# Openings of four stages prepared one stage earlier, and logits of a tree tile alternated with the outputs of the last one

## The chip, the cores and the metric

The kernel runs on one core of one Trainium2 chip. The metric is device time in microseconds (us), the median of three runs. A core has a matrix engine (TensorE, PE in the profile; its weight loads are shown as PEld), VectorE (DVE), ScalarE (ACT), GpSimd (POOL) and SyncE (SP), which here issues all DMA transfers. The engines run their own instruction streams and wait for each other through semaphores.

## The reference

Two transformer layers on x of shape (2, 1024, 128), all float32. In each, attention and feed-forward part read the same normalised x, and both are added to x:

```python
xn = layernorm(x)
x = x + attn0(xn) + moe(xn)      # 16 heads of 8, causal; 8 experts, top 2, hidden 512, gelu
xn = layernorm(x)
x = x + attn1(xn) + trees(xn)    # 16 query heads of 64 on 4 key heads, rotary, causal, top 64 scores
```

The tree part, which the change touches most:

```python
logits = x @ W_in.T + b_in                    # width 8 * 255: 8 binary trees of depth 7
decisions = (logits > 0)                      # at each node: left or right
acts = silu(logits)
dmap = nodes on the path from the root        # 8 of 255 per tree
out = (acts * dmap) @ W_out.T
```

## The kernel before

`build_program` (L2182) builds six stages, each an `nc.Block()` with one instruction stream per engine and a barrier of all engines at its end. Their buffers are taken at the start of a stage and given back at its end, except those in `g`, which live longer:

1. `project_layer0` (L109): layer norm, q and k of the first attention as three bf16 parts (written to DRAM by SyncE), v, router logits.
2. `attend_layer0` (L245): 32 heads. Its VectorE stream first clears q, k, v, nil and none (L654 to L661), counting on the semaphore `blank`; SyncE loads the first heads' q and k after `blank` 2 (L351), PE starts after `blank` 4 (L531).
3. `run_experts` (L667): router on VectorE, then 4 chunks of 512 tokens by 8 experts, PE and ScalarE (gelu) in turn. SyncE loads the tables of the trees at its start (L691 to L695); GpSimd has nothing to do.
4. `project_layer1` (L799): SyncE loads ten tables (L873), PE waits for all (L895), then for 16 tiles turns the attention output, multiplies it with wo and adds biases (L904 to L912), VectorE adds the sums to x. Then layer norm, v, and rotated q and k for the second attention, with GpSimd adding the two products of each rotation (L1098). VectorE clears v1, keys and second first (L1019 to L1021).
5. `walk_trees` (L1999): the trees, 16 tiles of 128 tokens.
6. `attend_layer1` (L1188): 32 heads in a software pipeline written out by hand. SyncE loads q, k and v of two heads, then seven tables (L1351); PE, GpSimd and VectorE wait for all seven (`table_in`), PE and ScalarE also for VectorE's clearing of the upper halves of q and k (`blank`).

In `walk_trees` VectorE first splits the bias `b_in` into three bf16 parts that sum to it (L2134 to L2137, on one partition), and SyncE moves these by DMA into three partitions (`bins`, L2030); PE waits for them. Then for each tile t: PE computes the logits in four chunks of 512 columns, two chunks to a half (`logits`, L2052); VectorE thresholds each half (`dec`, L2143), walks seven levels to get the path (L2151, L2152) and multiplies the activations with it ("masking", L2159, semaphore `masked`); ScalarE makes the activations of each half (`silu`, L2105). PE then turns the masked activations in four groups (`turn`, L2072, into ps_t), ScalarE copies each group to mT (`turned`, L2113), and PE multiplies it with W_out (L2083, `outputs`); VectorE adds the result to x (L2164). The order of each engine is written out: PE does logits(t), then outputs(t-1); ScalarE does both silus of t, then the four copies of t-1; VectorE does walk(t), then add(t-1). An instruction stream is in order, so that what stands behind a wait waits too.

## Time and profile before

| | |
|---|---|
| median of 3 runs | 2088.07 us (2087.74 to 2088.33) |
| profiled execution | 2088.2 us, its span 2086.5 |
| mean granted TensorE clock | 0.93 of full speed |
| PE / DVE / ACT / POOL busy | 84% / 72% / 64% / 30% of the span |

The span runs from the first to the last instruction of the trace; times in rows are counted from its start. Busy time is the union of an engine's instructions. The granted clock has two levels here, 1.00 (2.4 GHz) and 0.50 (1.2 GHz). In the profile's names `a_` is an attention stage, `p_` a projection, `ex_` the experts, `ff_` the trees, `g_` and `l_` buffers that live longer. A row of the order of time shows start, duration, engine, line, operation, output and inputs, count of merged instructions, and in square brackets how long the engine had been idle and who released it.

### The profile page before, as it was taken

What the parts mean: (1) busy time and instruction counts of PE and PEld (TensorE: products, weight loads), DVE (VectorE), ACT (ScalarE), POOL (GpSimd) and SP (SyncE); (2) the same over time, 40 slices, a digit from 0 to 9 for tenths busy, and PEclk for the clock granted to TensorE, in tenths of its full rate; (3) what the DMA queues carried; (4) which work ended last, traced back from release to release, by engine and by line L of the source; (5) the groups of instructions that cost most, each with busy time, mean ns of one, the idle gap of its engine ahead of it and who ended that gap; (6) DMA issues with size and microseconds to landing.
All of it is one profiled execution on the core that took longest, in us unless ns stands there. A gap on an engine that the chain in (4) does not pass through costs nothing. (4 is left out here: it accounts for less than half of the span.)

```text
span 2086.5 us, 35986 instructions
## 1 busy us (share of the span) xinstructions
PE 1760.6 (84%) x10131; PEld 1056.3 (51%) x10163; DVE 1497.3 (72%) x4721; ACT 1327.3 (64%) x2819; POOL 619.0 (30%) x1540
## 2 busy tenths in 40 slices
PE   5699999999978895888865888888889838988877
PEld 2345555577756443555532555555555525555544
DVE  4588888311133555777747899999999969999974
ACT  3177777533321521233347999999999939999983
POOL 0045454000000441000014444444444414444440
PEclk8599999999985997999987999999999969999988
DMA  6200000100010220000020110111100101011000
GB/s 168 82 21 22 23 23 16 41 1 0 0 50 0 81 91 31 0 0 0 0 64 11 31 32 16 31 31 31 31 24 23 31 16 28 18 31 31 21 18 15
DMA packets 38186, 61.77 MB, mean 30 GB/s; under 512 B 10225, under 2 KB 15347, under 8 KB 38004
## 3 DMA queue, kind: packets, MB, share of 16 engines
q1 hardware_dynamic: 38069, 60.51, 9.8%
q8 instruction: 36, 0.59, 0.1%
q14 instruction: 81, 0.66, 0.1%
HBM read 34.14 MB, written 17.83 MB: 25 GB/s over the span
## 5 line engine op out<-in xcount | busy, mean ns | idle before, releaser
L1629 ACT ACTIVATE a_trash<-a_sc,a_search 128x1024 bf16<-128x1024 f32 (+7 forms) x768 | 586.2, 767 | 74.6 <-POOL a_search L1568 31.7
L1384 PE MATMUL a_ps_s<-a_k,a_q 128*128 128x512 f32 (+3 forms) x768 | 311.1, 520 | 64.4 <-DVE a_sc L1845 51.1
L1418 PE MATMUL a_ps_o<-a_kT,a_v 128*65 128x512 f32 (+3 forms) x768 | 287.5, 498 | 53.7 <-ACT a_kT L1646 52.5
L1402 PE MATMUL a_ps_t<-g_ident,a_sc 128*128 128x128 f32 x1152 | 228.5, 285 | 20.9 <-ACT a_kT L1646 18.9
L1845 DVE TENSOR_SCALAR_CACHE_REDUCE a_sc<-a_ps_s,g_search 128x1024 f32<-128x1024 f32 (+7 forms) x256 | 207.9, 812 | 23.3 <-PE a_ps_s L1386 16.1
L585 DVE TENSOR_REDUCE a_top<-a_ps_row 128x1 f32<-128x512 f32 (+3 forms) x384 | 196.7, 553 | 24.6 <-PE a_ps_row L423 18.9
L1384 PEld LDWEIGHTS a_ps_s<-a_k,a_q 128*128 128x128 f32 x768 | 132.3, 196 | 160.0 <-issue 100.6
L1805 DVE SCALAR_TENSOR_TENSOR a_below<-a_sc,a_found 128x768 f32<-128x768 f32 (+7 forms) x256 | 211.3, 835 | 1.1
L1404 PE MATMUL a_ps_t<-a_minus,a_short 128*128 128x128 bf16 x1152 | 211.8, 221 | 0.0
L1402 PEld LDWEIGHTS a_ps_t<-g_ident,a_sc 128*128 128x128 f32 x1152 | 164.5, 143 | 92.0 <-ACT a_kT L1646 47.1
L549 ACT ACTIVATE a_prob<-a_ps_col 128x1024 f32<-128x1024 f32 (+7 forms) x256 | 159.2, 650 | 68.7 <-PE a_ps_col L436 65.5
L1646 ACT ACTIVATE a_kT<-a_ps_t 128x512 f32<-128x512 f32 x288 | 162.0, 583 | 24.9 <-PE a_ps_t L1404 17.7
L1418 PEld LDWEIGHTS a_ps_o<-a_kT,a_v 128*65 128x65 f32 x768 | 89.0, 140 | 164.5 <-ACT a_kT L1646 103.3
L741 ACT ACTIVATE ex_hid<-ex_ps_h,le_b 128x512 f32<-128x512 f32 x128 | 87.5, 687 | 128.1 <-PE ex_ps_h L718 127.8
L1818 DVE MAX8 a_best<-a_below 128x8 f32<-128x160 f32 (+5 forms) x576 | 157.2, 328 | 1.1
L1629 ACT ACTIVATION_READ_ACCUMULATOR a_trash<-a_sc,a_search 128x1 f32 x768 | 148.0, 193 | 0.0
L792 DVE SCALAR_TENSOR_TENSOR l_acc<-ex_ps_y,l_comb,l_acc 128x128 f32 x112 | 31.9, 345 | 151.4 <-PE ex_ps_y L709 151.1
L1639 ACT ACTIVATE a_short<-a_sc,a_cutoff 128x128 bf16<-128x128 f32 (+2 forms) x192 | 110.8, 655 | 44.9 <-DVE a_cutoff L1865 44.9
L1404 PEld LDWEIGHTS a_ps_t<-a_minus,a_short 128*128 128x128 bf16 x1152 | 123.7, 107 | 19.4 <-issue 19.4
L709 PEld LDWEIGHTS ex_ps_y<-le_w,ex_hid 128*128 128x128 f32 x1024 | 118.7, 192 | 13.4 <-issue 13.4
L709 PE MATMUL ex_ps_y<-le_w,ex_hid 128*128 128x128 f32 x1024 | 118.8, 275 | 0.0
L420 PE MATMUL a_ps_row<-a_k,a_q 128*128 128x512 bf16 (+3 forms) x353 | 114.7, 335 | 4.8 <-DVE a_top L585 2.7
(267 smaller groups left out, 3336.1 us busy)
## 6 DMA issues: line engine op xcount, KB each, us to landing
a_v<-g_v SPq DMA_DIRECT2D x32, 260.0 KB, 2.3
q1turned<-p_full SPq DMA_DIRECT2D x32, 256.0 KB, 2.0
a_q<-q1turned SPq DMA_DIRECT2D x32, 256.0 KB, 3.6
a_k<-k1turned SPq DMA_DIRECT2D x32, 256.0 KB, 4.0
stack<-p_parts SPq DMA_DIRECT2D x24, 256.0 KB, 3.7
a_q<-stack SPq DMA_DIRECT2D x32, 96.0 KB, 2.2
a_k<-stack SPq DMA_DIRECT2D x32, 96.0 KB, 2.2
le_w<-d_w SPq DMA_DIRECT2D x1, 2048.0 KB, 8.5
```

What stands on the lines that cost most here:

```text
L549: act.activation(prob[:, p, PO[j]:PO[j] + S - j * P], ps_col[:, col_buffer(n, p, j), 0:S - j * P], ACT.Exp, scale=SCALE).then_inc(col_read, 1)
L585: dve.tensor_reduce(top[:, i, c:c + 1], ps_row[:, bank, 0:width], AX.X, ALU.max).then_inc(row_read, 1)
L709: m = pe.matmul(ps_y[:, e % 2, t, :], hid[:, e % 2, hc, t * P:(t + 1) * P], w2[:, e, hc, :], start=(hc == 0), stop=(hc == HC - 1))
L1384: pe.matmul(ps_s[:, j % 2, c:c + w], q[:, p, i * P:width], k[:, p, c:c + w], start=True, stop=True)
L1402: pe.matmul(out, columns(h, i)[:, c * P:(c + 1) * P], g.ident[:, :], is_transpose=True, start=True, stop=False)
L1404: m = pe.matmul(out, short[:, OFF[i] + c * P:OFF[i] + (c + 1) * P], minus[:, :], start=False, stop=True)
L1418: m = pe.matmul(ps_o[0:VW1, lo // HALF, (lo % HALF) * P:CH], v[:, p, c, :], kT[:, u % 2, a * P:b * P], start=(c == 0), stop=(c == LAST[lo ...
L1629: act.activation(trash[:, u % 2, 0:(i + 1) * P], columns(h, i), ACT.Sign, scale=-1.0, bias=trials[:, p, c, i:i + 1], accum_out=balance[:, ...
L1646: act.activation(kT[:, u % 2, :], ps_t[:, u % 2, :], ACT.Exp).then_inc(t_read, 1)
L1805: lane[i] = did(dve.scalar_tensor_tensor(lows(i), columns(hs, i), found[:, i:i + 1], columns(hs, i), ALU.is_le, ALU.mult))
L1818: did(dve.max(best[:, p, i, a, :], buf[:, a * w:(a + 1) * w]))
L1845: dve.tensor_scalar(columns(h + 1, i), ps_s[:, j % 2, 0:(i + 1) * P], shift.rearrange("p n i -> p (n i)"), None, ALU.subtract, ALU.max, ac ...
```

## The change

Nothing of what is computed changes. Five parts:

- First attention: its buffers q, k, v, nil and none become `g.q0`, `g.k0` and so on, and GpSimd clears them in the stage before. VectorE keeps one small memset.
- Second projection: wo, bo and b2 are loaded in the experts (`mix_in`), and PE waits for these three only, and for the other seven tables ahead of v. The three memsets go from VectorE to GpSimd; VectorE waits for them ahead of its copies of v.
- Trees: the split of the bias is made in the experts by GpSimd, and SyncE moves the parts there.
- Second attention: maskq is loaded behind the first head's q and k, with a semaphore of its own, and is all that PE waits for, beside the clearing, of which GpSimd does k and VectorE q. The other six tables are waited for in the section of head 0 (GpSimd, VectorE) and head 1 (PE).
- Trees, the order: in the section of tile t, PE does the two chunks of the first half and one of the second, waits for the masking of t-1, turns the first group of t-1, does the last chunk of t, and then the remaining turns and outputs of t-1. ScalarE puts the two silus of t between the copies of t-1. VectorE's order stays.

```diff
@@ project_layer0 @@
+
+            @block.gpsimd
+            def _(pool):
+                pool.memset(g.q0[:, :, :], 0.0).then_inc(g.blank0, 1)
+                pool.memset(g.k0[:, :, :], 0.0).then_inc(g.blank0, 1)
+                pool.wait_ge(g.blank0, 2)
+                pool.memset(g.k0[SHIFT0:SHIFT0 + NSH, :, :], 1.0).then_inc(g.blank0, 1)
+                pool.wait_ge(g.blank0, 3)
+                pool.memset(g.v0_padded[:, :, :, :], 0.0).then_inc(g.blank0, 1)
+                pool.memset(g.nil[:, :], 0.0).then_inc(g.blank0, 1)
+                pool.memset(g.none[:, :], 0.0).then_inc(g.blank0, 1)
+                pool.wait_ge(g.blank0, 6)
@@ attend_layer0 @@
-                sp.wait_ge(blank, 2)
+                sp.wait_ge(blank, 6)
...
-                pe.wait_ge(blank, 4)
+                pe.wait_ge(blank, 6)
...
-                set_up = Chain(dve, blank)
-                dve.memset(q[:, :, :], 0.0)
-                dve.memset(top[:, :, :], -3.0e38)
-                set_up(dve.memset(k[:, :, :], 0.0))
-                set_up(dve.memset(k[SHIFT0:SHIFT0 + NSH, :, :], 1.0))
-                set_up(dve.memset(v[:, :, :, :], 0.0))
-                dve.memset(none[:, :], 0.0)
-                set_up(dve.memset(nil[:, :], 0.0))
+                Chain(dve, lowest)(dve.memset(top[:, :, :], -3.0e38))
@@ run_experts @@
+                sp.dma_start(g.bin32[:, :], g.d_bin).then_inc(g.trees_in, 16)
+                for dst, src in ((g.wo0, g.d_wo0), (g.bo0, g.d_bo0), (g.b2, g.d_b2)):
+                    sp.dma_start(dst[:, :], src).then_inc(g.mix_in, 16)
                 sp.dma_start(g.win[:, :], g.d_win).then_inc(g.trees_in, 16)
-                sp.dma_start(g.bin32[:, :], g.d_bin).then_inc(g.trees_in, 16)
...
+                sp.wait_ge(bias_ready, 4)
+                for part in range(3):
+                    sp.dma_start(g.bins[part:part + 1, :], binp[0:1, part, :]).then_inc(g.bins_in, 16)
+                sp.wait_ge(g.bins_in, 48)
+
+            @block.gpsimd
+            def _(pool):
+                pool.wait_ge(g.trees_in, 64)
+                b = Chain(pool, bias_ready)
+                b(pool.tensor_copy(binp[0:1, 0, :], g.bin32[0:1, :]))
+                b(pool.tensor_tensor(rest[0:1, :], g.bin32[0:1, :], binp[0:1, 0, :], ALU.subtract))
+                b(pool.tensor_copy(binp[0:1, 1, :], rest[0:1, :]))
+                b(pool.tensor_tensor(binp[0:1, 2, :], rest[0:1, :], binp[0:1, 1, :], ALU.subtract))
@@ project_layer1 @@
-                pe.wait_ge(w_in, 16 * 10)
+                pe.wait_ge(g.mix_in, 16 * 3)
...
+                pe.wait_ge(w_in, 16 * 7)
...
-                pe.wait_ge(blank, 1)
+                pe.wait_ge(blank, 3)
...
-                dve.memset(g.v1[:, :, :, :], 1.0)
-                dve.memset(keys[:, :, :, :, P:P + 1], 1.0)
-                dve.memset(second[:, :, :, :, :], 0.0).then_inc(blank, 1)
...
+                dve.wait_ge(blank, 3)
...
-                pool.wait_ge(w_in, 16 * 10)
+                pool.memset(g.v1[:, :, :, :], 1.0).then_inc(blank, 1)
+                pool.memset(keys[:, :, :, :, P:P + 1], 1.0).then_inc(blank, 1)
+                pool.memset(second[:, :, :, :, :], 0.0).then_inc(blank, 1)
+                pool.wait_ge(blank, 3)
+                pool.wait_ge(w_in, 16 * 7)
@@ attend_layer1 @@
 
                 load(0, 0)
+                sp.dma_start(maskq[:, :], g.d_maskq1).then_inc(mask_in, 16)
+                for dst, src in ((wide[:, :], g.d_wide), (limit[:, :], g.d_limit), (ceiling[:, :], g.d_ceiling)):
+                    sp.dma_start(dst, src).then_inc(table_in, 16)
                 load(1, 1)
                 load_v(0, 0)
                 load_v(1, 1)
-                for dst, src in ((iota.rearrange("p s j -> p (s j)"), g.d_rank), (wide[:, :], g.d_wide),
-                                 (maskq[:, :], g.d_maskq1), (minus[:, :], g.d_minus), (ceiling[:, :], g.d_ceiling), (limit[:, :], g.d_limit),
+                for dst, src in ((iota.rearrange("p s j -> p (s j)"), g.d_rank), (minus[:, :], g.d_minus),
                                  (wo.rearrange("p h w -> p (h w)"), g.d_wo1)):
                     sp.dma_start(dst, src).then_inc(table_in, 16)
...
+                    if is_at(n, 1):
+                        pe.wait_ge(table_in, 16 * 6)
...
-                pe.wait_ge(blank, 3)
-                pe.wait_ge(table_in, 16 * 7)
+                pe.wait_ge(blank, 2)
+                pe.wait_ge(mask_in, 16)
...
                     if is_at(n, -1):
+                        after(did(pool.memset(k[DH1:P, :, :], 0.0)))
+                        pool.sem_inc(blank, 1)
                         did(pool.memset(inverse[:, :], -1.0))
-                        pool.wait_ge(table_in, 16 * 7)
+                    if is_at(n, 0):
+                        pool.wait_ge(table_in, 16 * 6)
                         after(did(pool.tensor_scalar(wide_aim[:, :], wide[:, :], AIM, None, ALU.add)))
...
                     if is_at(n, -1):
-                        did(dve.memset(q[DH1:P, :, :], 0.0))
-                        did(dve.memset(k[DH1:P, :, :], 0.0))
-                        after(made[0])
-                        dve.sem_inc(blank, 3)
-                        dve.wait_ge(table_in, 16 * 7)
+                        dve.memset(q[DH1:P, :, :], 0.0).then_inc(blank, 1)
                         did(dve.memset(best[:, :, NARROWEST:TB, QUARTERS, 7:8].rearrange("p b s e -> p b (s e)"), TINY))
+                    if is_at(n, 0):
+                        dve.wait_ge(table_in, 16 * 6)
                         did(dve.tensor_scalar(least[:, 0:NARROWEST], limit[:, 0:NARROWEST], TINY, None, ALU.mult))
@@ walk_trees, tensor @@
+
+                def half(t, p, x):
+                    for c, w in BOUNDS[2 * x:2 * x + 2]:
+                        pe.matmul(ps_l[:, c:c + w], g.onesb[0:3, :], bins[:, c:c + w], start=True, stop=False)
+                        yield pe.matmul(ps_l[:, c:c + w], xt[:, p, :], win[:, c:c + w], start=False, stop=True)
+
...
+                def logits(t, p, first, x, both):
                     pe.wait_ge(x_ready, t + 1)
-                    for x in range(2):
-                        if not (first and p == 0):
-                            pe.wait_ge(silu_ready, t * 2 + (x - 1))
-                        for c, w in BOUNDS[2 * x:2 * x + 2]:
-                            pe.matmul(ps_l[:, c:c + w], g.onesb[0:3, :], bins[:, c:c + w], start=True, stop=False)
-                            m = pe.matmul(ps_l[:, c:c + w], xt[:, p, :], win[:, c:c + w], start=False, stop=True)
-                        m.then_inc(l_ready, 1)
-
-                def outputs(t, p, first):
-                    pe.wait_ge(masked, t + 1)
-                    if not (first and p == 0):
-                        pe.wait_ge(f_read, t)
-
-                    def turn(x):
-                        if not (first and p == 0 and x < 2):
-                            pe.wait_ge(t_read, t * NCK + (x - 1))
-                        for c in range(4 * x, min(4 * x + 4, NCH)):
-                            w = P if c < NCH - 1 else LASTW
-                            m = pe.transpose(ps_t[0:w, x % 2, (c % 4) * P:(c % 4 + 1) * P],
-                                             act_v[:, p, c * P:c * P + w], g.ident[:, :])
-                        m.then_inc(t_ready, 1)
-
-                    turn(0)
-                    for x in range(NCK):
-                        if x + 1 < NCK:
-                            turn(x + 1)
-                        pe.wait_ge(t_read, t * NCK + (x + 1))
-                        for c in range(4 * x, min(4 * x + 4, NCH)):
-                            w = P if c < NCH - 1 else LASTW
-                            m = pe.matmul(ps_f[:, 0:P], mT[0:w, x % 2, (c % 4) * P:(c % 4 + 1) * P],
-                                          wout[0:w, c, :], start=(c == 0), stop=(c == NCH - 1))
-                        if x == NCK - 1:
-                            m.then_inc(f_ready, 1)
-
-                logits(0, 0, True)
-                logits(1, 1, True)
-                outputs(0, 0, True)
+                    if not first:
+                        pe.wait_ge(silu_ready, t * 2 + (x - 1))
+                    chunks = half(t, p, x)
+                    next(chunks)
+                    if both:
+                        next(chunks).then_inc(l_ready, 1)
+                    return chunks
+
+                def section(t, p, first):
+                    u, q = t - 1, 1 - p
+                    logits(t, p, False, 0, True)
+                    second = logits(t, p, False, 1, False)
+                    pe.wait_ge(masked, t)
+                    turn(u, q, first, 0)
+                    next(second).then_inc(l_ready, 1)
+                    turn(u, q, first, 1)
+                    output(u, q, first, 0)
+                    turn(u, q, first, 2)
+                    output(u, q, first, 1)
+                    turn(u, q, first, 3)
+                    output(u, q, first, 2)
+                    output(u, q, first, 3)
+
+                logits(0, 0, True, 0, True)
+                logits(0, 0, True, 1, True)
+                section(1, 1, True)
                 with pe.Fori(1, NT // 2) as i:
-                    logits(i * 2, 0, False)
-                    outputs(i * 2 - 1, 1, False)
-                    logits(i * 2 + 1, 1, False)
-                    outputs(i * 2, 0, False)
-                outputs(NT - 1, 1, False)
+                    section(i * 2, 0, False)
+                    section(i * 2 + 1, 1, False)
+                pe.wait_ge(masked, NT)
+                turn(NT - 1, 1, False, 0)
+                for x in range(NCK):
+                    if x + 1 < NCK:
+                        turn(NT - 1, 1, False, x + 1)
+                    output(NT - 1, 1, False, x)
 
@@ walk_trees, scalar @@
+                def section(t, p, first):
+                    u = t - 1
+                    turned(u, 0)
+                    silu(t, p, first, 0)
+                    turned(u, 1)
+                    silu(t, p, first, 1)
+                    turned(u, 2)
+                    turned(u, 3)
+
+                silu(0, 0, True, 0)
+                silu(0, 0, True, 1)
+                section(1, 1, True)
@@ walk_trees, vector @@
-                b = Chain(dve, bias_ready)
-                b(dve.tensor_copy(binp[0:1, 0, :], bin32[0:1, :]))
-                b(dve.tensor_tensor(rest[0:1, :], bin32[0:1, :], binp[0:1, 0, :], ALU.subtract))
-                b(dve.tensor_copy(binp[0:1, 1, :], rest[0:1, :]))
-                b(dve.tensor_tensor(binp[0:1, 2, :], rest[0:1, :], binp[0:1, 1, :], ALU.subtract))
-                b(dve.memset(path[:, :, 0:1], 1.0))
+                dve.memset(path[:, :, 0:1], 1.0).then_inc(bias_ready, 1)
+                dve.wait_ge(bias_ready, 1)
```

## Rows read from the trace of the kernel before

**Rows 1.** Stretches of the six stages: length, busy time by engine, clock, DMA share, GB/s.

```profile
0.00:69.00 69.00, 44.67 (x128) 28.39 (x128) 27.81 (x90) 18.26 (x30) 0.19 (x4) 0.74 0.60 174
69.00:383.00 314.00, 288.30 (x2267) 147.18 (x2299) 256.66 (x675) 217.72 (x321) 135.91 (x316) 0.96 0.08 21
383.00:612.00 229.00, 225.54 (x1288) 163.92 (x1288) 42.47 (x150) 90.01 (x131) 0.00 (x0) 1.00 0.03 10
612.00:813.00 201.00, 164.96 (x752) 91.69 (x752) 104.55 (x223) 57.04 (x144) 61.57 (x50) 0.82 0.18 66
813.00:1056.00 243.00, 191.10 (x960) 123.08 (x960) 168.95 (x301) 69.79 (x113) 5.72 (x17) 0.91 0.00 1
1056.00:2086.00 1030.00, 846.05 (x4736) 502.04 (x4736) 896.90 (x3285) 874.45 (x2081) 415.56 (x1153) 0.95 0.10 27
```

**Rows 2.** Order of time around the opening of the first attention.

```profile
74.59 3.47 DVE L658 MEMSET a_k<- 3x4096 bf16 x1 [0.91 <-DVE a_k L657]
...
78.49 0.41 SPq L349 DMA_DIRECT2D a_k<-stack  x1
...
81.02 0.29 PE L420 MATMUL a_ps_row<-a_k,a_q 128*128 128x128 bf16 x1 [0.69 <-DMA a_k<-stack]
```

**Rows 3.** Order of time, opening of the second projection.

```profile
623.52 0.48 PE L899 MATMUL p_ps_a<-g_ident,l_o 128*128 128x128 f32 x1 [12.80 <-DMA p_quantile<-d_quantile]
...
623.55 3.72 POOL L1103 TENSOR_SCALAR p_wqk<-p_wqk 128x1024 f32<-128x1024 f32 x1 [243.28 <-DMA p_quantile<-d_quantile]
...
627.24 2.76 POOL L1103 TENSOR_SCALAR p_wqk_rot<-p_wqk_rot 128x1024 f32<-128x1024 f32 x1
```

**Rows 4.** Order of time, opening of the trees.

```profile
816.19 1.51 POOL L2039 COPY ff_xt<-l_xnT 128x128 f32<-128x128 f32 x2 [18.50 <-POOLq L870]
...
827.32 0.58 PE L2058 MATMUL ff_ps_l<-ff_bins,g_onesb 3*128 3x512 bf16 x1 [17.03 <-DMA ff_bins<-ff_binp]
```

**Rows 5.** Opening of the second attention: order of time, then DMA issues (KB, us to landing).

```profile
1054.43 0.58 SPq L1339 DMA_DIRECT2D a_k<-k1turned  x1
...
1066.12 1.19 PE L1384 MATMUL a_ps_s<-a_k,a_q 128*128 128x512 f32 x1 [12.88 <-DMA a_wo<-d_wo]
...
a_k<-k1turned SPq DMA_DIRECT2D x2, 256.0 KB, 4.8
```

**Rows 6.** One tree tile in order of time.

```profile
869.24 0.38 PE L2058 MATMUL ff_ps_l<-ff_bins,g_onesb 3*128 3x512 bf16 x1
...
870.61 0.39 PE L2058 MATMUL ff_ps_l<-ff_bins,g_onesb 3*128 3x512 bf16 x1
...
873.45 1.22 DVE L2143 TENSOR_SCALAR ff_dec<-ff_ps_l 128x1016 bf16<-128x1016 f32 x1 [1.50 <-PE ff_ps_l L2059]
...
876.26 1.16 PE L2083 MATMUL ff_ps_f<-l_wout,ff_mT 128*128 128x128 f32 x8 [1.97 <-ACT ff_mT L2113]
...
880.10 2.29 DVE L2159 TENSOR_TENSOR ff_act_v<-ff_act_v,ff_path 128x2040 f32<-128x2040 f32 x1
...
882.39 0.39 PE L2058 MATMUL ff_ps_l<-ff_bins,g_onesb 3*128 3x512 bf16 x1
```

**Rows 7.** Trees: all maskings, who waited for them, first outputs, last 6.8 us.

```profile
L2159 DVE TENSOR_TENSOR ff_act_v<-ff_act_v,ff_path x16: 2282/2284/2285, 841.6 to 1044.5; 128x2040 f32<-128x2040 f32 x16
...
  PE ff_ps_t L2072: 5.1, 2
...
843.96 1.97 PE L2072 MATMUL ff_ps_t<-g_ident,ff_act_v 128*128 128x128 f32 x8 [3.52 <-DVE ff_act_v L2159]
...
854.72 0.38 PE L2058 MATMUL ff_ps_l<-ff_bins,g_onesb 3*128 3x512 bf16 x1
...
1046.80:1053.60 6.80, 5.89 (x48) 5.45 (x48) 0.47 (x2) 2.34 (x5) 0.00 (x0) 1.00 0.01 2
```

**Rows 8.** Stretches around the opening of the second projection: the clock is the third last number.

```profile
605.00:610.00 5.00, 5.00 (x48) 5.00 (x47) 1.13 (x4) 0.00 (x0) 0.00 (x0) 1.00 0.00 0
...
623.50:659.30 35.80, 35.64 (x128) 26.66 (x128) 5.46 (x22) 8.04 (x33) 6.45 (x2) 0.50 0.00 1
```

More of the change, by code:

```diff
@@ L253, in attend_layer0 @@
         GW = P // GR
[L254 to L258 removed]
+        q, k, v, nil, none = g.q0, g.k0, g.v0_padded, g.nil, g.none
         top = r.sb("top", [P, TB, 2])
@@ new lines, in turn, with output @@
+                def turn(t, p, first, x):
+                    if not (first and x < 2):
+                        pe.wait_ge(t_read, t * NCK + (x - 1))
+                    for c in range(4 * x, min(4 * x + 4, NCH)):
+                        w = P if c < NCH - 1 else LASTW
+                        m = pe.transpose(ps_t[0:w, x % 2, (c % 4) * P:(c % 4 + 1) * P],
+                                         act_v[:, p, c * P:c * P + w], g.ident[:, :])
+                    m.then_inc(t_ready, 1)
+                def output(t, p, first, x):
+                    if x == 0 and not first:
+                        pe.wait_ge(f_read, t)
+                    pe.wait_ge(t_read, t * NCK + (x + 1))
+                    for c in range(4 * x, min(4 * x + 4, NCH)):
+                        w = P if c < NCH - 1 else LASTW
+                        m = pe.matmul(ps_f[:, 0:P], mT[0:w, x % 2, (c % 4) * P:(c % 4 + 1) * P],
+                                      wout[0:w, c, :], start=(c == 0), stop=(c == NCH - 1))
+                    if x == NCK - 1:
+                        m.then_inc(f_ready, 1)
@@ L2129, in _ @@
+                for x in range(NCK):
+                    turned(NT - 1, x)
             @block.vector
```

95 lines of the change are left out of this document (43 added, 52 removed).

## The prediction, made before the change was run

> **What bounds the kernel now.** I read the kernel as six stages that run one after another, each closed by a barrier of all engines, and the first view is the busy time and clock of those six stretches [rows 1]. The reader is to see that no engine bounds all of it: TensorE (PE) is near full in the experts (225.5 of 229 us), VectorE and ScalarE share the last stage (896.9 and 874.5 of 1030), and in the other stages PE has gaps. The second view is the order of time around each barrier, where one looks for what the first useful instruction of a stage waited for. Four of the five openings have a hole in which PE does nothing: 69 to 81.0, 612.5 to 623.5, 816.2 to 827.3 and about 1054 to 1066.1 [rows 1 to 5]. The experts have none. The third view is one tile of the tree stage: there PE, not VectorE, is the fuller engine, and it stands still once a tile, 1.97 us, for ScalarE [rows 6].
>
> The profiled execution took 2088.2 us, its span 2086.5, the median of the runs 2088.07. I make the sum against 2088.2 (span plus 1.7).
>
> **Opening of the first attention.** VectorE clears q, k, the shift rows, v, none and nil, and SyncE loads q and k only after the third of these. The first score matmul comes at 81.02, 2.5 us after the k load was issued at 78.49 [rows 2]. With the buffers cleared by GpSimd a stage earlier, SyncE can issue right behind the barrier. The stage before ends at 69 [rows 1]; I take the q load at 69.2, the k load half a microsecond behind it, at 69.7, and the first matmul at 72.2. That is 8.8 us. The six GpSimd memsets that are added lie in a stage in which GpSimd does nothing. No row shows a large memset there: VectorE writes 4096 elements in 3.47 us [rows 2], GpSimd's tensor_scalar does 1024 in 2.76 [rows 3]. Between these ends the six take 12 to 39 us, and the stage lasts 69, so they are covered at either end; without that cover they would cost what exceeds 69. What is not excluded is that they slow VectorE's layer norm: 0 to 2 us, and I take 0.5, since the wait for x fills most of the time in which they run.
>
> **Opening of the second projection.** PE waits for ten tables, the last landed at 623.5 [rows 3]. After the change PE needs wo, bo and b2, which were loaded during 229 us of experts, so it starts behind the barrier; the experts end at 612 [rows 1], and I take 613.1, 10.4 us saved. VectorE's three memsets go to GpSimd, ahead of its two scalings. By the same two rates they take 7 to 22 us, and the scalings 6.5; GpSimd is then free at about 641 on the old clock, and its first rotation and VectorE's v copies, which now wait for these memsets, come near 660 after the shift. So the new wait costs nothing; the residual additions, which stand behind the memsets on VectorE, start that much sooner. The seven other tables land at about 623 and are first wanted by PE at about 660.
>
> Beside VectorE's additions GpSimd's first scaling took 3.72 us, and the second, the same shape, 2.76 [rows 3]: the two engines do hinder each other here. The Trainium skill, page "SBUF — State Buffer", section "Who interferes with whom", has GpSimd and VectorE lock a shared port pair for a whole instruction, which speaks against moving memsets to GpSimd; it also says that a GpSimd instruction that only writes does not meet an addition with two inputs. By the first half the sum would lose at most some 3 us per stage, by the second nothing.
>
> **Opening of the trees.** GpSimd has the tile of xn ready at about 816.9; PE starts at 827.32 because the bias is split into three bf16 parts by four VectorE instructions and then moved by DMA [rows 4]. All of this now runs in the experts on GpSimd and SyncE, which have no other work there after their loads. 10.4 us saved; three small loads are put before the win load, which nobody needs for 400 us.
>
> **Opening of the second attention.** PE waits for seven tables, of which wo is issued last, and starts at 1066.12 when it has landed [rows 5]. After the change it waits for q, k and maskq, issued as the first three. The k load, issued at 1054.43, with the 4.8 us to landing that such loads take in this stretch, gives 1059.2, and less when it has no four loads behind it: I take 1058.8, 7.3 us saved. GpSimd clears the upper half of k meanwhile: 2048 elements, by the two rates above 1.7 to 5.5 us from the same moment on, at worst 1 us later than the landing. The wait for wo moves to the section of head 0 on GpSimd and VectorE, and to head 1 on PE; the eight score tiles of head 0 keep them until about 1071, so it costs nothing.
>
> Openings together: 8.8 + 10.4 + 10.4 + 7.3 - 0.5 = 36.4 us.
>
> **The tree stage.** A tile at full clock takes 13.15 us (869.24 to 882.39), of which PE stands 1.97 for the first mT copy [rows 6], as ScalarE does both silus of the next tile before it. So PE's own work is 11.2 us. The stage's average is longer: between the first and the last masking, which start at 841.6 and 1044.5 [rows 7], lie 202.9 us for 15 tiles, 13.5 each. The new order puts the second logits chunk of half 1 behind the first transposes and lets ScalarE copy between the silus. A new loop arises: the masking ends, the first four transposes (0.5, half clock takes 1.97 for eight [rows 7]), the last chunk (869.24 to 870.61, 1.4), threshold, paths and masking on VectorE, which take 873.45 to 882.39, 8.9 [rows 6]. With 0.3 for the handover that is 11.1 us, just within PE's 11.2. Behind PE's wait for the masking stand the last chunk and all output work of the tile before, and VectorE waits for that chunk; ScalarE has 69.8 / 16 = 4.4 us of work in a tile [rows 1] and is not late. So a tile takes 11.2 us if nothing else is added.
>
> Start and end are worse than that. After the first masking PE runs at half clock; it had stood 3.5 us [rows 7], and from 843.96 to 854.72 did the outputs of one tile, 10.8 us. In the new order this stretch loses the 1.8 us wait, gains a chunk of 2.7 at half clock and is followed by three chunks of 1.4: 15.8 us until PE is ready for the second masking. Then 13 tiles at 11.2, then 10.8 to the last masking: 172.2 us in place of 202.9, 30.7 saved. At the end PE now stands about 3.7 us for the last masking, where it stood 1.6 (the two waits for a masking make 5.1, of which 3.5 is the first one), and the outputs of the last tile, 6.8 us at full clock [rows 7], may take the 10.8 of half clock: I charge 4.0. Net 26.7 us; bounds are 31 (no charge) and 14 (a tile at 12.2, say by handovers that I don't see).
>
> **Sum.** 36.4 + 26.7 = 63.1 us, so 2088.2 - 63.1 = 2025.1 us.
>
> **Rivals.** (B) The clock is kept in the second projection. From 623.5 to 659.3 PE is busy all the time and yet at half clock [rows 8], 2.2 us for each of 16 tiles; before the hole it had full clock. Without the hole it enters at full clock. At double the clock it could lose at most 17.9 of its 35.8 us, and the gaps between instructions don't shrink with it; I take 15: 2010 us. Against it: 35 us of this very mix never raised the clock. I take it as falling back soon, with no gain. The Trainium skill, page "TensorE: Matmul & The Clock Gate", section "HAM oscillation", has only long idle gaps throttle the engine, and by that rule the clock would be kept; that is this rival. (C) The new loop in the trees binds above PE's work: each tile pays two more handovers or a late chunk, 12.4 us a tile, 14 x 1.2 = 17 us more: 2042. For it: the loop of 11.1 and PE's 11.2 are so close that any jitter adds. (E) One opening is not won, because another wait stands behind the removed one (the q and k loads, GpSimd's memset of k): some 8 us, 2033. This is the case in which the change does not do all it says. (D) Slower than before: in the trees the last chunk is held until the outputs are done, for example because ScalarE's copies wait for silus which wait for thresholds. A tile is then PE's 11.2 and VectorE's 8.9 in series, 20.1: (20.1 - 11.2) x 14 = 125 us more, 2150. It decides the sign from a tile above 15.7 us; against it stands that the chunk is issued ahead of every wait for a copy.
>
> **How the numbers follow.** Forecast 0.52 (2018 to 2031), B 0.20, C 0.13, E 0.11, D 0.04. The range from 2006 to 2037 leaves out C and D, 0.17. About 0.2% (4 us) can be told from no change; all cases but D are far beyond it: faster 0.95, same 0.01, slower 0.04.
>
> **What would show it.** First score matmul of the first attention near 72; first transposes of the second projection near 604, and their clock (0.50 or 1.00) decides between forecast and B; first bias matmul of the trees within 1 us of its barrier; a masking every 11.2 us, with PE's wait for the mT copy gone; the first score matmul of the last stage about 5 us behind its barrier. The prediction is wrong if the masking comes every 12 us or more, if VectorE waits over 1 us for the second half of the logits, or if the last stage (1030 us) changes in more than its opening.

## The result and the profile after

The changed kernel took 2020.15 us (median of 4 runs, 2017.26 to 2024.22) beside 2088.20 for the kernel before (2087.74 to 2088.66). The ratio is 0.9676, with a 95% interval from 0.9655 to 0.9696: 68 us, or 3.2%, faster. The prediction was 2025, with a range from 2006 to 2037. The profiled execution took 2017.26 us, its span 2015.5; against the profiled one of before that is 70.9 us less, where the sum had 63.1. One execution in the last round of experiments (5825 us) and one of the kernel before beside it (4334 us) were disturbed and stand in no figure here.

First the same six stages as in [rows 1], cut at the changed kernel's own borders. The columns are the stretch, its length, and for each engine the busy time and the number of instructions, then TensorE's granted clock, the DMA share and GB/s.

```profile
0.00:68.60 68.60, 43.55 (x128) 28.00 (x128) 28.19 (x90) 18.26 (x30) 12.56 (x10) 0.73 0.61 175
68.60:377.00 308.40, 294.87 (x2307) 148.12 (x2307) 249.16 (x673) 218.68 (x321) 136.01 (x316) 0.97 0.08 21
377.00:603.00 226.00, 224.45 (x1280) 163.07 (x1280) 41.43 (x146) 89.06 (x130) 11.85 (x4) 1.00 0.03 10
603.00:795.50 192.50, 162.96 (x752) 90.83 (x752) 99.76 (x226) 56.92 (x144) 71.37 (x53) 0.83 0.19 68
795.50:991.50 196.00, 186.03 (x960) 116.17 (x960) 156.09 (x289) 70.41 (x113) 4.62 (x16) 0.95 0.00 0
991.50:2015.50 1024.00, 847.00 (x4736) 502.83 (x4736) 896.65 (x3284) 874.08 (x2081) 418.22 (x1155) 0.95 0.10 27
```

The experts and the body of the last stage are as before. The tree stage went from 243 us to 196, with TensorE busy for 186 of them, and its clock from 0.91 to 0.95. GpSimd has 12.56 us in the first stage and 11.85 in the experts, where it had almost nothing [rows 1]: that is the moved work.

Second, what the first useful instruction of each stage waited for. The rows are of the timeline of the changed kernel: start, duration, engine, line, operation; in brackets the idle time before and what ended it. They answer to [rows 2 to 5].

```profile
68.15 0.29 DVE L204 COPY l_logits<-p_ps_r 128x128 f32<-128x128 f32 x1 [6.63 <-PE p_ps_r L253]
71.71 0.29 PE L428 MATMUL a_ps_row<-le_k,le_q 128*128 128x128 bf16 x1 [2.33 <-DMA le_k<-stack]
...
603.29 3.56 POOL L1116 MEMSET g_v<- 128x4160 f32 x1 [202.83 <-POOLq L691]
603.33 0.30 PE L915 MATMUL p_ps_a<-g_ident,l_o 128*128 128x128 f32 x1 [1.73 <-PEq L691]
603.33 3.32 DVE L1038 TENSOR_TENSOR g_x<-g_x,l_acc 128x128 f32<-128x128 f32 x16 [0.32 <-PEq L691]
606.88 7.12 POOL L1118 MEMSET p_second<- 128x8192 bf16 x1
...
796.15 0.58 PE L2069 MATMUL ff_ps_l<-l_bins,g_onesb 3*128 3x512 bf16 x1 [6.34 <-POOL ff_xt L2054]
...
991.82 1.80 POOL L1618 MEMSET a_k<- 64x2048 f32 x1 [38.78 <-POOLq L2047]
996.71 1.19 PE L1405 MATMUL a_ps_s<-a_k,a_q 128*128 128x512 f32 x1 [5.58 <-DMA a_maskq<-d_maskq]
```

TensorE's holes of 12.80 and 17.03 us [rows 3, 4] are now 1.73 and 6.34, and what is left of the second is mostly the end of the stage before. The last stage begins 5.26 us behind the last tree addition, now on the landing of maskq and no longer on wo.

Third, one tile of the tree stage, from one masking on VectorE (L2193) to the next. It answers to [rows 6].

```profile
837.04 2.29 DVE L2193 TENSOR_TENSOR ff_act_v<-ff_act_v,ff_path 128x2040 f32<-128x2040 f32 x1
838.28 1.12 PE L2070 MATMUL ff_ps_l<-l_win,ff_xt 128*128 128x512 f32 x2
839.47 0.65 PE L2077 MATMUL ff_ps_t<-g_ident,ff_act_v 128*128 128x128 f32 x4
840.05 0.38 PE L2069 MATMUL ff_ps_l<-l_bins,g_onesb 3*128 3x504 bf16 x1
840.16 0.60 ACT L2143 ACTIVATE ff_mT<-ff_ps_t 128x512 f32<-128x512 f32 x1 [6.08 <-PE ff_ps_t L2077]
840.36 1.11 PE L2070 MATMUL ff_ps_l<-l_win,ff_xt 128*128 128x504 f32 x2
841.31 0.60 PE L2077 MATMUL ff_ps_t<-g_ident,ff_act_v 128*128 128x128 f32 x4
841.51 1.22 DVE L2177 TENSOR_SCALAR ff_dec<-ff_ps_l 128x1016 bf16<-128x1016 f32 x1 [0.85 <-PE ff_ps_l L2070]
841.75 1.06 PE L2087 MATMUL ff_ps_f<-l_wout,ff_mT 128*128 128x128 f32 x8
...
848.15 2.28 DVE L2193 TENSOR_TENSOR ff_act_v<-ff_act_v,ff_path 128x2040 f32<-128x2040 f32 x1
```

The copy that TensorE waited 1.97 us for runs from 840.16 to 840.76, beside the last chunk (L2069 and L2070, 840.05 to 841.47); the output matmuls that need it start at 841.75 without a wait. The tile takes 11.11 us. Two loops could set this time: the one from masking to masking over the chunk and VectorE's walk, and TensorE's own work. TensorE has no gap at all: the masking ends at 839.33, and TensorE's last matmul before the transposes that need it at 839.40. In the later tiles the masking is 0.14 to 0.17 us ahead, so TensorE's work binds, by that little. The same stretch by windows, with the first rise and the drain around it:

```profile
813.00:820.00 7.00, 4.73 (x15) 2.86 (x16) 4.42 (x3) 1.73 (x3) 0.29 (x1) 0.52 0.00 0
850.00:981.00 131.00, 129.82 (x713) 83.49 (x711) 114.61 (x216) 51.87 (x84) 2.93 (x10) 1.00 0.00 0
984.00:991.00 7.00, 7.00 (x48) 6.59 (x47) 0.00 (x0) 2.45 (x5) 0.00 (x0) 0.79 0.01 2
```

TensorE is busy for 129.8 of 131 us at a full clock. Before, the clock was at half for 3.4 us in every third tile, which took 14.8 us in place of 13.15.

### The profile page after: what moved, and what is told of

Read it like the earlier page. It is cut to its first block and busy times, and to the rows that moved or that the text cites. A ratio compares the mean times of both kernels' runs of the same rounds, so it can differ in the third digit from the quotient of the medians.

```text
span 2015.5 us, 36012 instructions
## 1 busy us (share of the span) xinstructions
PE 1758.9 (87%) x10163; PEld 1049.0 (52%) x10163; DVE 1471.3 (73%) x4707; ACT 1327.4 (66%) x2819; POOL 654.6 (32%) x1554
## 5 line engine op out<-in xcount | busy, mean ns | idle before, releaser
L428 PE MATMUL a_ps_row<-le_k,le_q 128*128 128x512 bf16 (+3 forms) x384 | 123.9, 340 | 6.5 <-DVE a_top L593 2.9
L393 POOL TENSOR_SCALAR_AFFINE_SELECT a_prob<-a_prob 128x128 f32<-128x128 f32 x256 | 75.2, 294 | 146.6 <-POOLq L390 145.9
```

Of the source, the lines that this page charges most:

```text
L428: last = pe.matmul(ps_row[:, bank, 0:width], q[:, h, i * P:(i + 1) * P], k[:, h, c * CH:c * CH + width], start=True, stop=True)
```

## The experiments

All were built from the changed kernel unless something else is said. "The mark" means the start of an instruction in the profile. Stages of one execution differ from those of another by a few us (last section), so causes are read from marks, and totals are given beside them. The kernel before was measured anew beside each of the three rounds and had medians of 2086.1, 2087.4 and 2087.5 us; a ratio is to the one of its own round.

**The two halves, one at a time.** In the first kernel the functions of TensorE and ScalarE in the trees are the old ones; in the second only they are new.

```diff
 # open_only: block tensor and block scalar of walk_trees
-                section(1, 1, True)
+                logits(1, 1, True)
+                outputs(0, 0, True)
 # order_only: before.py with these two blocks of the changed kernel
```

> The changed kernel with the old order of the tree stage on TensorE and ScalarE: the four openings alone. Theory (the two halves of the change add up): the trace of the changed kernel has the openings worth 9.3 + 10.9 + 10.8 + 7.4 = 38 us, so 2049 to 2051 us. As forecast in the prediction (36.4): 2052. Rival (part of the 31 us won in the trees comes only with the other half, for example because the clock is different when the trees start): under 2045 or over 2056. The trees themselves should again take a masking every 13.1 us with a dip of the clock every third tile.

> The kernel before with the new order of the tree stage alone, on TensorE and ScalarE. Theory (halves add up): 31 us by the trace of the changed kernel, so 2057; the prediction's term of 26.7 gives 2061. A masking every 11.1 us and no fall of the clock from the third tile to the last masking. Rival (the order needs the opening without a hole): less than 24 us won, over 2064.

Openings alone: 2054.0 us (2052.3 to 2054.5), ratio 0.9843 (0.9827 to 0.9860), span 2050.6. Order alone: 2054.3 (2052.2 to 2054.6), ratio 0.9841 (0.9825 to 0.9858), span 2052.4. By the spans, against 2086.5, the halves are worth 35.9 and 34.1 us, together 70.0, where both at once gave 71.0: they add up. The ratios say the same: 1.57% and 1.59% less, against 3.24% for both (3.14% when measured again below). The median of the first lies 3 us above the band of its theory; in its profile the first stage ended at 70.34 in place of 68.44, which is 1.9 of them. The second is 3 us under its theory, the better side. The tree stage keeps to itself: with the old order a masking came every 13.13 us and every third after 14.8, with the new one every 11.11 even without the better opening.

```profile
845.00:1015.00 170.00, 144.35 (x753) 94.97 (x752) 123.64 (x230) 53.95 (x89) 3.17 (x11) 0.96 0.00 0
```

(This is the tree stage of the first kernel: TensorE has 144 us of work in 170, and the clock is 0.96.)

**Which engine's order matters.** One engine's order is put back, the other's is left new.

```diff
 # act_old: ScalarE
...
-                    section(i * 2, 0, False)
+                    silu(i * 2, 0, False)
+                    turned(i * 2 - 1, 1, False)
...
 # pe_old: TensorE
-                    section(i * 2, 0, False)
+                    logits(i * 2, 0, False)
+                    outputs(i * 2 - 1, 1, False)
```

> The changed kernel with ScalarE's old order in the trees (both silus ahead of all copies), TensorE's order new. Theory (ScalarE's order carries the gain): TensorE stands for the first copy until threshold 1.2, silu 1.0 and copy 0.6 have followed the last chunk, less 0.6 of transposes, some 2.3 us a tile, and the clock dips again: a masking every 13.3 to 14 us, 2052 to 2062 us. Rival (TensorE's order carries it, the chunk behind the first transposes covers the copies): 2018 to 2026 us.

> The changed kernel with TensorE's old order in the trees (all four chunks of the logits ahead of the wait for the masking), ScalarE's order new. Theory (ScalarE's order carries the gain, and TensorE's work of 11.0 us a tile is the bound): a masking every 11.1 to 11.3 us, 2018 to 2026 us. Rival (the place of the last chunk is what covers the first copy): TensorE stands 1 us or more for it in each tile, and the time is 2032 or more. Second rival (the loop from masking to masking bound the new order, and is gone here): a masking every 10.97 us or a little less, 1 to 3 us faster than the changed kernel's 2017 to 2024.

ScalarE's order put back: 2054.9 us (2053.0 to 2056.2), a masking every 13.59. TensorE's order put back: 2024.05 (2022.2 to 2027.0), a masking every 11.50. The output matmul that waits for the first copy, in the one and in the other (start, duration, idle time before it):

```profile
920.43 1.16 PE L2087 MATMUL ff_ps_f<-l_wout,ff_mT 128*128 128x128 f32 x8 [2.41 <-ACT ff_mT L2145]
934.02 1.16 PE L2087 MATMUL ff_ps_f<-l_wout,ff_mT 128*128 128x128 f32 x8 [2.41 <-ACT ff_mT L2145]
```

```profile
922.07 1.16 PE L2098 MATMUL ff_ps_f<-l_wout,ff_mT 128*128 128x128 f32 x8 [0.25 <-ACT ff_mT L2126]
933.57 1.16 PE L2098 MATMUL ff_ps_f<-l_wout,ff_mT 128*128 128x128 f32 x8 [0.25 <-ACT ff_mT L2126]
```

So ScalarE's order carries the gain: with its old one, TensorE's new order is worth nothing (13.59 a tile, where both old give 13.5 on average). ScalarE's new order by itself takes the tile from 13.5 to 11.50 us. The chunk behind the first transposes is worth the last 0.4 us a tile: without it the copy is covered only by four transposes, and 0.25 us of it shows as idle time; the other 0.14 was not traced to anything. TensorE's old place of the chunk also takes the chunk out of the loop over VectorE, and the tile did not get shorter than 11.11. As it brought the 0.25 us wait with it, this run alone does not decide which loop binds; that is read from the changed kernel's own tile above. One part of the expectation failed: with 2.41 us of idle time in each tile the clock should have dipped again. It did not:

```profile
850.00:1019.00 169.00, 137.69 (x752) 89.22 (x752) 123.63 (x231) 54.39 (x90) 3.06 (x11) 1.00 0.00 0
```

The old order dips with a wait of 1.97 us in each tile, this one does not with 2.41. What tells them apart was not found.

**The second projection: tables or memsets?** Each of its two removed waits is put back alone.

```diff
 # mix_memsets_vector: on VectorE, ahead of its additions
...
-                pool.memset(second[:, :, :, :, :], 0.0).then_inc(blank, 1)
+                dve.memset(second[:, :, :, :, :], 0.0).then_inc(blank, 1)
...
 # mix_all_tables
                 pe.wait_ge(g.mix_in, 16 * 3)
+                pe.wait_ge(w_in, 16 * 7)
```

> The changed kernel with the three memsets of the second projection back on VectorE, ahead of its additions; all tables as changed. They take 3.5 + 0.1 + 3.5 us and 1 us of gaps. Theory (both halves of this opening were needed): TensorE starts behind the barrier, but stands from its third tile on, since VectorE's first residual addition comes 8 us later and PSUM has room for two tiles; 6 to 8 us lost, 2024 to 2030 us. Rival (the tables alone were the hole, the memsets were hidden): within 2 us of the changed kernel, 2017 to 2024 us.

> The changed kernel, but TensorE waits for all seven tables of the second projection at its start, as before; memsets stay on GpSimd. Theory (the early start is what was won): the first transposes come when the last table has landed, 9 to 11 us behind the barrier, 2027 to 2033 us. Rival (the start is made up for later in the stage, since what follows the 16 tiles waits for something else): 2017 to 2024 us.

Memsets back: 2024.95 us (2022.9 to 2026.1). Tables back: 2030.8 (2030.2 to 2036.3). TensorE in the first and then in the second, with two rows of the first kernel's other engines:

```profile
613.96 4.09 DVE L1041 TENSOR_TENSOR g_x<-g_x,l_acc 128x128 f32<-128x128 f32 x16
617.61 3.07 POOL L1121 TENSOR_SCALAR p_wqk_rot<-p_wqk_rot 128x1024 f32<-128x1024 f32 x1
618.40 0.77 PE L926 MATMUL p_ps_b<-l_wo,p_oT 128*128 128x128 f32 x2 [7.63 <-DVE g_x L1045]
```

```profile
614.71 0.45 PE L916 MATMUL p_ps_a<-g_ident,l_o 128*128 128x128 f32 x1 [10.88 <-DMA p_quantile<-d_quantile]
```

With the memsets back TensorE started at once and then stood 7.63 us; from its first transpose to the norms it took 43.8 us in place of 35.5, 8.3 more. With the tables back it stood 10.88, and from the first matmul of the experts to the norms 273.1 us passed in place of 261.7, 11.4 more. Two causes thus lay behind one hole, and either alone would have kept most of it. Of the 7.63 us some 0.8 are not the memsets but the additions behind them, which ran beside GpSimd's scalings and took 4.09 us in place of 3.3. In the medians 3 to 5 of the 8.3 us show. In its profiled execution the next stretch was 3.4 us shorter (159.6 in place of 163.0 from the first v copy to the first masking, last section), other stretches were longer, and the span is 8.7 us above that of the changed kernel; totals do not settle a cause of this size.

**The clock in the second projection (rival B).** In this loop TensorE is never idle and runs at half clock. The first kernel gives it denser work, the second only at the start.

```diff
 # mix_dense; dense_start and bias_row_start: only for t < 4
+                    pe.matmul(ps_q[:, 0, :], g.ident[:, :], g.xnT[:, 0:CH], start=True, stop=True)
                     pe.matmul(out, oT[:, t % 2, :], wo[:, :], start=True, stop=False)
```

> The changed kernel with one more matmul of 128 rows by 512 columns in fp32 in each of the 16 tiles of the second projection's first loop (into a PSUM bank that is free there; its result is not used). TensorE's clock is 0.50 there and stays so for 35 us of small matmuls. Theory A (the operands of the loop, of 1, 8 and 128 rows by 128 columns, are what keeps the clock low, and denser work raises it within some tiles): the loop takes about 2.2 us a tile after the first ones (1.1 for the old work at full clock, 1.13 for the new matmul), total within 8 us of the changed kernel's 2020. Theory B (what the matmuls hold does not matter, the clock stays low): 4.3 us a tile, 33 us more, 2050 to 2056.

> The changed kernel with the one extra matmul (128 rows, 512 columns, fp32, result unused) in tiles 0 to 3 of the second projection's first loop only; with it in all 16 the clock was full from the third tile. Theory (the small matmuls do not raise the clock and do not keep it either): it falls again within some tiles, 2.19 us a tile from then on, 2022 to 2030 us. Rival (this is the prediction's case B: once full, the clock stays full in this mix): from tile 4 on 1.1 to 1.4 us a tile, norms start 4 to 7 us sooner than in the changed kernel, 2012 to 2017 us.

With it in all tiles: 2023.5 us (2018.9 to 2029.6). The first tiles, from transpose to transpose, took 4.2, 3.9 and 3.7 us, all later ones 2.09. With it in four: 2016.95 (2016.6 to 2027.9). The tiles took 4.5, 3.55, 2.09 and 2.09, then seven came every 1.23 us, one took 1.84, and from there on 2.19 again. Windows of the first kernel, then of the second:

```profile
605.00:615.00 10.00, 9.89 (x24) 5.64 (x24) 3.09 (x15) 1.22 (x7) 9.91 (x4) 0.52 0.71 255
616.00:643.00 27.00, 27.00 (x129) 17.30 (x128) 3.74 (x13) 6.37 (x25) 4.47 (x2) 1.00 0.00 1
```

```profile
606.00:613.00 7.00, 6.71 (x18) 3.61 (x16) 3.38 (x17) 1.16 (x6) 7.00 (x3) 0.54 0.87 300
620.00:627.00 7.00, 7.00 (x48) 5.54 (x47) 1.73 (x6) 2.23 (x11) 2.04 (x1) 1.00 0.00 0
627.00:637.00 10.00, 9.96 (x37) 7.41 (x35) 1.15 (x5) 2.97 (x9) 0.00 (x0) 0.50 0.01 2
```

The first fits theory A: with denser work the clock rose, and from then on a tile with the added matmul took 2.09 us, where one without it takes 2.19 in the changed kernel. The second is the test of rival B. The clock was full for 13.6 us, the last 9.8 of them with small matmuls alone, and then fell with no gap ahead of it (7.00 of 7 us busy). By total and by the start of the norms (4.0 us sooner behind the first transpose) this kernel meets the numbers of case B and not those of the theory, as seven quick tiles paid for the added work; but the clock is not kept, which is what the theory said.

**Shorter work in that loop.** The bias bo becomes the ninth row of b2, against a row of ones in the transposed weights, which saves one matmul in each tile.

```diff
 # bias_row
-                for dst, src in ((g.wo0, g.d_wo0), (g.bo0, g.d_bo0), (g.b2, g.d_b2)):
+                for dst, src in ((g.wo0[:, :], g.d_wo0), (g.b2[NE:NE + 1, :], g.d_bo0), (g.b2[0:NE, :], g.d_b2)):
...
-                    pe.matmul(out, g.ones[0:1, :], bo[0:1, :], start=False, stop=False)
                     pe.matmul(out, cT[:, t % 2, :], b2[:, :], start=False, stop=True).then_inc(sum_ready, 1)
...
```

> The changed kernel, with bo as a ninth row of b2 and a row of ones in the transposed weights, so that the 16 two-pass matmuls of one row are gone from the second projection's first loop. By the trace of the changed kernel a tile is 2.19 us, of which these take 0.4 to 0.55 (two weight loads of 0.25 and the gaps). Theory (the loop is bound by TensorE at half clock): 16 x 0.5 = 8 us less, 2009 to 2016. Rival 1 (ScalarE's copies bind as soon as TensorE is shorter, oT to oT is 2.19 now): 0 to 3 us less. Rival 2 (the one-row matmuls are also what keeps the clock low): the clock rises within the loop, 1.2 us a tile, 14 to 16 us less, 2001 to 2007.

> The same extra matmul in tiles 0 to 3, on the kernel without the one-row matmuls (bo as ninth row of b2). Theory, as before: the clock falls again, 1.77 us a tile, 5 us more than that kernel's 2010: 2013 to 2018. Rival (case B): 0.9 to 1.2 us a tile from tile 4 on, 2 to 5 us less than it: 2004 to 2009. If the one-row matmuls alone made the difference between kept and lost, the clock stays full here and falls in the kernel with them.

Without the added work: 2010.4 us (2001.0 to 2012.0), ratio 0.962 (0.959 to 0.965). By its median this is the fastest kernel of the study: its slowest execution is 5 us ahead of the changed kernel's fastest (2017.3). A tile takes 1.77 us in place of 2.19, 0.42 x 16 = 6.7 us less, and its clock stayed at half in the profile; so the theory holds, and in that execution taking the one-row matmuls away did not raise the clock. The median fell by 10 to 12 us, more than the edit is worth: in the profile another 4.3 us come from the stretch behind it, from the first v copy to the first masking (last section). With the four denser matmuls: 2011.2 (2004.1 to 2017.8), in the profile 2016.1 of span. There the clock stayed at half to the end of the loop, the tiles took 3.5 and then 1.77 us, and neither theory foresaw it: the same four matmuls had raised it in the profile of the kernel above.

Here one profile does not stand for the kernel, as the mean granted clocks of its other executions show. The two of this last kernel that took 2015.6 and 2017.8 us (the profiled one) had 0.942, the two that took 2004.1 and 2006.9 had 0.948 and 0.947. One less the clock, times the span, is what the lower clock can have cost: 117 us in the first two, 104 and 106 in the others, about as much apart as their times. With dense_start it is the other way about: the three at 2016.6 to 2017.3 us, the profiled one among them, had 0.943 or 0.944, and one at 2027.9 had 0.939. So the same code runs with one clock or another, and in the executions without a profile the four matmuls may have done the opposite. That is not shown, and what decides it stays open.

**The changed kernel once more.**

> The changed kernel once more, for its spread and for a second profile of the same code. Theory (the spread of 7 us between its executions comes from when TensorE's clock falls and rises around the second projection and at the start of the trees, not from the code): times between 2016 and 2026, median 2018 to 2024; the stretch from the first v copy to the first bias matmul of the trees 144 to 149 us, that from there to the first masking either about 14.5 or about 16.7 us. Rival (the spread comes from the first stage's loads or the last stage): these two stretches as in the first profile (146.2 and 16.8) within 0.3 us, and a difference elsewhere.

Five executions took 2018.4 to 2024.3 us, ratio 0.9686 (0.9673 to 0.9699), 65 us below the kernel before, where the first measurement had 68. The profile (span 2017.6) has 148.3 us from the first v copy to the trees' first matmul and 14.5 from there to the first masking, as the theory had it; in the first profile they were 146.2 and 16.8. But their sum is the same (162.8 and 163.0), so they do not explain the spread; the 2.0 us between these two profiles lie mostly in the last stage (1.3), from the first to the last masking (0.4) and in the fourth opening (0.4). The executions of 2022 to 2024 us have no profile. Their mean granted clock was 0.936 to 0.938, against 0.939 or 0.940 in those of 2017 to 2019. For the first four executions one less the clock, times the span, gives 123 us for the two quick ones and 127 and 129 for the others, about what they are apart in time. So the theory's cause, the clock, is borne out by these numbers; its place, around the second projection and the start of the trees, is not, and stays open.

## Why the prediction was right, step by step

The table gives each stretch between two marks in the profiled executions.

| stretch, up to | before | after | won | forecast |
|---|---|---|---|---|
| first score matmul | 81.02 | 71.71 | 9.3 | 8.3 |
| first transpose of the second projection | 542.50 | 531.62 | 10.9 | 10.4 |
| first bias matmul of the trees | 203.80 | 192.82 | 11.0 | 10.4 |
| first masking | 14.30 | 16.78 | -2.5 | 0 |
| last masking | 202.89 | 168.55 | 34.3 | 30.7 |
| end of the last tree addition | 9.05 | 9.97 | -0.9 | -4.0 |
| first score matmul of the last stage | 12.56 | 5.26 | 7.3 | 7.3 |
| end of the span | 1020.38 | 1018.79 | 1.6 | 0 |
| sum | 2086.5 | 2015.5 | 71.0 | 63.1 |

**Openings.** All four went as forecast within 1 us. The 0.5 us charged for a slower layer norm was not due: the first stage ended at 68.44, before it was 68.95. Of GpSimd's memsets I had two bounds, from a VectorE memset and from GpSimd's tensor_scalar [rows 2, 3]; the time came near the lower one. 4096 elements take 3.51 us in the first stage, 4160 take 3.56, so the six take 12.6 us in sum (bounds 12 and 39). The three of the second projection took 11.1 (bounds 7 and 22): the bound of 7 counted `second` as 4096 words, as VectorE writes it, and GpSimd wrote 8192 bf16 elements in 7.12 us. These are over at 614.0, long before the v copies at 650, and the one of k in the last stage at 993.6, 3.1 us ahead of the first score matmul. No mark shows a cost of them, also beside VectorE: the 16 additions that ran beside a GpSimd memset took 3.32 us, before the change 3.25.

What I had weighed there can be read from two meetings. In the kernel with the memsets back on VectorE the same 16 additions met GpSimd's scalings and took 4.09 us, and the scalings 2.92 and 3.07 where they take 2.78 alone. In the kernel before, the additions (621.38 to 624.63) met the first scaling for their last 1.1 us; they took 3.25 us, and the scaling 3.72, so there GpSimd lost 0.96 us and VectorE nothing that shows. The Trainium skill, page "SBUF — State Buffer", section "Who interferes with whom", has a VectorE instruction with two SBUF inputs meet a GpSimd instruction that reads SBUF, and not one that only writes it; the traces agree on both parts. The section calls the pair of ports that they share "an exclusive lock": the 0.96 of 1.1 us come near to that, the additions slowed by a quarter do not, and no run here tells why.

**Trees.** The tile was forecast at 11.2 us from TensorE's own work and at 11.1 from the new loop; it takes 11.11, with TensorE never idle, so its work is the one that binds. Rival C (12.4 a tile, by handovers of a loop so near to the bound) did not come: from the third tile on, up to the last, the masking ended 0.07 to 0.17 us before TensorE was ready for it. How close this was shows in a sign that I had named: VectorE waits 0.85 us in each later tile for the second half of the logits, where over 1 us was to speak against me; in the second and third tile it waited 2.58 and 1.12. Rival D (a tile above 15.7) had no part. The terms that failed were those at the ends. I had given the first interval 15.8 us, the drain 4.0 more than before and the last interval 10.8; they took 12.66, 0.9 and 11.09. My step took half clock for the whole of such a stretch because it stood so in [rows 7]. Here the clock was at half only from 812.9 to 819.7, and for 3.4 us in the drain. The 15.8 was also TensorE's time until it is ready for the second masking, and I used it as the time between maskings. TensorE's took 13.2 us; the second masking came by VectorE's way over the late chunk, 0.6 us before TensorE was ready for it. On the other side is a charge that I didn't have, 2.5 us for the first tile's logits, which ran at half clock. Together the trees gave 30.9 us where I had 26.7; this is 4.2 of the 7.8 us by which the sum fell short, and the openings (38.5 in place of 36.4) and the last stage make up the rest. That the net error is so small is in part luck: two charges of 3 us too many stand against one of 2.5 that was missing.

**The rest.** 1.6 us in the last stage is not the change: over the thirteen profiles of this study it took between 1018.4 and 1020.4 us from its first score matmul. Rival E (an opening not won) fell with the marks. Against the medians the error is smaller, 2020.15 and 2025.1: the profiled execution was one of the quick ones.

**Rival B**, to which I gave 0.20, did not come. TensorE entered the stage at full clock 1.73 us after its last expert matmul, and fell to half 1.4 us later, for the rest of the loop:

```profile
603.30:604.30 1.00, 0.67 (x5) 0.39 (x5) 0.97 (x5) 0.52 (x4) 1.00 (x1) 1.00 0.02 6
604.30:638.00 33.70, 33.70 (x123) 25.70 (x124) 6.58 (x27) 7.41 (x31) 15.22 (x5) 0.51 0.21 75
```

The reason against it in the prediction, that 35 us of this mix never raised the clock, pointed the right way but was weaker than it looked, since not rising is not falling; dense_start shows the missing half, a fall out of this very mix. The Trainium skill, page "TensorE: Matmul & The Clock Gate", section "HAM oscillation", puts such falls down to gaps in which TensorE has no work. The fall itself has a gap of 1.73 us shortly ahead of it; what no gap explains is the rest of the loop, 33.7 of 33.7 us busy at half clock, and the fall in dense_start.

## What to carry to other kernels

Look at every barrier for what the first instruction behind it waits for, and count all the waits there: the second projection had two behind one hole, and removing only the one on the tables would have won 3 us of 11, and only the one on the memsets nothing. Where an engine serves two loops (here the silus of the next tile and the copies of the last one), put the short piece for which the bound engine stands first: that by itself was worth 2.0 us in each of 15 tiles (2.5 beside TensorE's new order), while reordering the bound engine gave 0.4 on top and nothing by itself. When a tile falls to the work of one engine, its ends deserve the same care as the tile, since the clock there was not the one that the old kernel shows. And where executions of one kernel spread by 7 to 14 us, read the granted clock of each of them before one profile is taken for the kernel.

## What the hardware showed that was not expected

A TensorE that is busy all the time may stay at half clock (0.50 for 35 us of matmuls of at most 128 columns, which is 1.2 of 2.4 GHz), and in the profile with one fp32 matmul of 512 columns more in each tile it went to full (2.09 us a tile with it, 2.19 without). The same kind of clock difference moves stages that no edit touches: from the first v copy to the first masking of the trees the same instructions took 162.6 to 163.0 us in eight profiles and 158.5 to 159.6 in three. One of each, with its mean clock of 0.91 and 0.94:

```profile
649.97:812.93 162.96, 137.63 (x627) 64.64 (x625) 89.62 (x156) 49.80 (x110) 55.96 (x51) 0.91 0.18 65
```

```profile
643.89:802.58 158.69, 133.66 (x627) 63.42 (x625) 89.57 (x156) 49.84 (x110) 56.01 (x51) 0.94 0.18 67
```

(The first row is of the changed kernel, the second of bias_row.) VectorE's, ScalarE's and GpSimd's busy times agree within 0.1 us, TensorE's differ by 4.0. The three came with edits ahead of the stretch; whether the edit or the execution decides was not tested. Either way such a stretch can hide or double the effect of an edit of a few us, which is better judged by its own marks than by the total. GpSimd's memset took 0.86 to 0.87 us per 1000 elements of a partition, in fp32 and in bf16 alike (3.56 us for 4160 and 7.12 for 8192); VectorE's cleared the same 8192 bf16 elements in 3.47 us, written as 4096 words of 32 bits.
